# Graph attention on one core: combines moved behind the head, second maxima joined later, their store contiguous

## The reference

```python
seq = (x @ W_seq).reshape(N, H, DH)
score1 = jnp.einsum('nhd,d->hn', seq, a1)
score2 = jnp.einsum('nhd,d->hn', seq, a2)
scores = score1[:, :, None] + score2[:, None, :]
scores = jax.nn.leaky_relu(scores, negative_slope=ALPHA)
scores = scores + (1.0 - adj)[None, :, :] * MASK_VAL
attn = jax.nn.softmax(scores, axis=-1)
hidden = jnp.einsum('hij,jhd->ihd', attn, seq).reshape(N, D_IN)
hidden = hidden @ W_out + b_out
return jax.nn.elu(hidden)
```

## Time and profile before

| | us |
|---|---|
| median of 3 runs | 518.84 (518.45 to 519.27) |
| the profiled execution's own time | 522.9 |
| its span, first to last instruction | 521.2 |
| TensorE busy | 503.4 (97%) |
| VectorE busy | 459.6 (88%) |
| ScalarE busy | 433.7 (83%) |
| GpSimd busy | 34.8 (7%) |

### The profile page before, as it was taken

How to read it: one execution, slowest core, us unless ns; L and a number is a source line. 1 busy time by engine, 2 the same in 40 slices (tenths; PEclk the granted TensorE clock), 3 DMA queues, 4 the chain that set the end, 5 groups by cost and what they waited for, 6 DMA issues and landing times.

```text
span 521.2 us, 15251 instructions
## 1 busy us (share of the span) xinstructions
PE 503.4 (97%) x6744; PEld 456.7 (88%) x6744; DVE 459.6 (88%) x577; ACT 433.7 (83%) x462; POOL 34.8 (7%) x64
## 2 busy tenths in 40 slices
PE   7999999999999989999999999999999999899993
PEld 5788889999999889999999999999999999644542
DVE  3266899998999898999999999999998879988886
ACT  2477899798999887999999999999995989356664
POOL 3000000000000010000000000000000000035444
PEclk9899999999999989999999999999999999999998
DMA  7999995202020411201021120202202040015343
GB/s 258 395 302 344 333 332 142 86 3 82 3 83 2 115 38 55 83 3 82 3 83 31 54 83 3 83 1 83 79 7 82 3 143 3 1 62 159 122 141 122
DMA packets 31617, 53.28 MB, mean 102 GB/s; under 512 B 19392, under 2 KB 20672, under 8 KB 27584
## 3 DMA queue, kind: packets, MB, share of 16 engines
q1 hardware_dynamic: 31000, 51.79, 30.5%
q10 hardware_dynamic: 552, 0.52, 0.3%
HBM read 43.78 MB, written 4.33 MB: 92 GB/s over the span
## 4 chain that ended last, share of the span: by engine, by line
PE 80%; DVE 9%; DMA 4%; ACT 3%; issue 2%; POOL 0%; ACTq 0%; POOLq 0%; DVEq 0%
PE sums L475 35%; PE bank L489 19%; PE sums L568 10%; PE sums L400 6%; PE sums L416 4%; DVE tring L816 3%; ACT tring L614 2%; DVE tring L811 2%; DMA maxima<-Vp 2%; PE sums L387 1%; PE bank L416 1%; PE bank L556 1%; DMA Vp<-in_L_gnn_W_seq_dram 1%; DMA Vp<-maxima 1%; DVE Vp L792 1%
## 5 line engine op out<-in xcount | busy, mean ns | idle before, releaser
L614 ACT ACTIVATE tring<-abc,ab 128x2048 int8<-128x2048 f32 x150 | 292.2, 2019 | 2.0 <-PE sums L475 2.0
L475 PE MATMUL sums<-Vp,tring 128*128 128x132 f16 x4096 | 241.8, 221 | 3.5 <-issue 2.4
L475 PEld LDWEIGHTS sums<-Vp,tring 128*128 128x128 fp8e4 x4096 | 236.9, 98 | 5.5 <-issue 3.5
L816 DVE TENSOR_TENSOR tring<-adj,tring 128x1024 uint32<-128x1024 uint32 (+1 forms) x134 | 155.9, 1174 | 13.6 <-ACT tring L614 9.1
L489 PE MATMUL bank<-Vp,adj 128*128 128x132 f16 x2048 | 127.7, 222 | 2.1 <-DVE Vp L866 2.1
L489 PEld LDWEIGHTS bank<-Vp,adj 128*128 128x128 fp8e4 x2048 | 123.8, 97 | 2.3 <-DVE Vp L866 2.3
L811 DVE TENSOR_SCALAR tring<-abc,ab 128x2048 int8<-128x2048 f32 x90 | 115.5, 1283 | 0.0
L568 PE MATMUL sums<-abc,Vp 128*128 128x512 f32 (+1 forms) x136 | 57.5, 568 | 0.1
L568 PEld LDWEIGHTS sums<-abc,Vp 128*128 128x128 f32 x136 | 24.7, 190 | 22.7 <-issue 22.0
L652 ACT ACTIVATE low<-sums 128x33 f32<-128x33 f32 (+3 forms) x66 | 20.1, 393 | 24.1 <-PE sums L475 24.0
L592 ACT ACTIVATE tring<-Vp 128x2048 int8<-128x2048 f32 x16 | 30.6, 1911 | 1.2 <-DMA Vp<-in_adj_dram 1.2
(11 more groups left out here) (116 smaller groups left out, 369.7 us busy)
## 6 DMA issues: line engine op xcount, KB each, us to landing
Vp<-in_adj_dram SPq DMA_DIRECT2D x16, 1024.0 KB, 8.1
abc<-a_rows SPq DMA_DIRECT2D x15, 1024.0 KB, 4.8
abc<-in_x_dram SPq DMA_DIRECT2D x16, 256.0 KB, 7.4
Vp<-in_x_dram SPq DMA_DIRECT2D x16, 256.0 KB, 2.9
out_dram<-Vp SPq DMA_DIRECT2D x16, 256.0 KB, 2.0
abc<-in_L_gnn_W_out_dram SPq DMA_DIRECT2D x1, 1024.0 KB, 5.3
Vp<-in_L_gnn_W_seq_dram ACTq DMA_DIRECT2D x2, 256.0 KB, 5.4
Vp<-in_L_gnn_W_seq_dram SPq DMA_DIRECT2D x2, 256.0 KB, 6.1
```

Source lines behind the costliest of these rows:

```text
L475: mm = pe.matmul(bank[b][:, c * 2 * VW:(c + 1) * 2 * VW], slot(jt)[:, it * P:(it + 1) * P].bitcast(F8), Vp[:, h, jt, :, :], start=(jt == 0 ...
L614: return act.activation(slot(jt)[:, columns], row(h)[:, columns], ACT.Sign, bias=ab[:, jt, H + h:H + h + 1], scale=-1.0)
L816: return dve.tensor_tensor(words, edges, words, ALU.bitwise_and)
```

## The change

Three edits:
- The store of the second maxima writes `scratch2` in the order (partition, head), so each partition writes 8 successive values instead of 8 scattered ones. The maximum then reads `peaks` as "(q h)", with a step of 8 values between elements.
- The wait for the maxima, the maximum and the powers go from tile 7 to tile 11 of head 4, and `scale_factors` from tile 10 to tile 13.
- The combine of head k, k = 0 to 7, goes from tiles 11, 12 and 13 of head k + 4 to tiles 0, 2 and 3 of head k + 5. From head 12 on the old places hold (heads 8, 9 and 10), so head 12 has two combines and head 4 none.

```diff
--- before.py
+++ after.py
@@ -71,7 +71,8 @@
 VALUES_AT, HIGH_AT, LOW_AT = 1, 6, 9
 
 BEHIND_AT = (None, (6, 8)) + (range(6, NT),) * (H - 3) + ((5, 6, 8, 9),)
-FINISH_AT = (11, 12, 13)
+
+FINISH_AT, SOON_AT, LATER = (11, 12, 13), (0, 2, 3), 12
 
 THREE_AT = (9, 11, 15)
 
@@ -346,7 +347,7 @@
                 if h == 5:
 
                     sp.wait_ge(mx2_ready, 1)
-                    sp.dma_start(scratch2.rearrange("o (h p) -> (o p) h", p=P), mx2, allow_slow_non_contiguous=True).then_inc(mx2_stored, 16)
+                    sp.dma_start(scratch2.rearrange("o (p h) -> (o p) h", p=P), mx2).then_inc(mx2_stored, 16)
                     sp.wait_ge(mx2_stored, 16)
                     sp.dma_start(peaks, scratch2[0:1, :].partition_broadcast(P)).then_inc(peaks_loaded, 16)
                 sp.dma_start(row(h), scratch[h:h + 1, :].partition_broadcast(P)).then_inc(abc_loaded[h % 2], 16)
@@ -977,12 +978,12 @@
                     if h == 3 and jt == 14:
                         dve.wait_ge(mx2_part, 4)
                         dve.tensor_reduce(mx2, mxd.rearrange("p c k -> p k c"), AX.X, ALU.max).then_inc(mx2_ready, 1)
-                    if h == 4 and jt == 7:
+                    if h == 4 and jt == 11:
                         dve.wait_ge(peaks_loaded, 16)
-                        dve.tensor_reduce(mx2, peaks.rearrange("p (h q) -> p h q", q=P), AX.X, ALU.max).then_inc(peak_made, 1)
+                        dve.tensor_reduce(mx2, peaks.rearrange("p (q h) -> p h q", q=P), AX.X, ALU.max).then_inc(peak_made, 1)
                         dve.wait_ge(peak_made, 1)
                         powers(slice(HALF, H), mx2, 1)
-                    if h == 4 and jt == 10:
+                    if h == 4 and jt == 13:
                         scale_factors(1, slice(HALF, H))
                     if h == 5 and jt == 0:
                         dve.wait_ge(e_scaled, 4)
@@ -992,6 +993,8 @@
                             finish(step, h - GRP, 1, h - GRP)
                         dve.wait_ge(fin_step, 3 * (h - GRP + 1))
                         inverse(0, slice(0, NT), slice(0, H - GRP))
+                    if GRP < h <= LATER and jt in SOON_AT:
+                        finish(SOON_AT.index(jt), h - GRP - 1, 1, h - GRP - 1)
                     if jt == SUMS_AT[h]:
                         dve.wait_ge(low_copied, h)
                         if h > GRP:
@@ -1004,7 +1007,7 @@
                         if jt == VALUES_AT:
                             dve.wait_ge(v_ready, k)
                             values(k)
-                    if GRP <= h < H - 1 and jt in FINISH_AT:
+                    if LATER <= h < H - 1 and jt in FINISH_AT:
                         finish(FINISH_AT.index(jt), h - GRP, 1, h - GRP)
                     if h == H - 1 and jt in THREE_AT:
                         dve.wait_ge(joined, h)
```

## The result

The changed kernel is slower: median 523.2 us of 7 runs (521.91 to 524.6) against 519.27 us before, ratio 1.008, 95% interval [1.0062, 1.0099]. The forecast was 517.1 us. One of the 7 runs of the kernel before took 1828 us, which its median leaves aside.

What follows compares the result with a forecast made beforehand. TensorE bounds the kernel, busy 503.4 of 521.2 us, so only its waits count: 5.29 - 0.17 - 3.32 - 1.58 = 0.22, plus 1.48 of small waits, gain 1.70 from 518.84: 517.1 us; range 515.4 to 521.2.

Steps and rivals of the forecast that it cites:

- Head 4 and 5: VectorE's join of sums at 198.5 lets TensorE start head 5 at 199.9 (201.73 before), after 3.3 us idle.
- The reduction: VectorE's maximum over 1024 values in head 4, now read with a stride: 2.10 us instead of 1.22, a cost of 0.88.
- Stall (a): TensorE's gap after one product of head 4, until the maxima's store lands: 1.20 us lost, taken as the store's.
- Piece (c): Head 4's 64 products over the edges at half clock after a wait: 5.37 us instead of 3.79, 1.58 lost.
- Part 4: Combines moved behind the head, still ahead of the next join of sums: the work of one VectorE cycle stays.
- the 1.48 of small waits: TensorE's waits for VectorE ahead of heads 6, 8, 10 and 12, 0.37 us first, 1.48 in all: expected to go.
- The dependence: Last combine step is followed at once by the join overwriting its cab slot: 0.13 us, between 0 and 0.18.
- the third rival: Head 4's wait exists only in the profiled execution; new kernel slower by 2.3 to 3.0 us, 521.1 to 521.8; chance 25%.
- the 4.06 us: Excess of the profiled execution over the median; the store of 1024 pieces was called a likely place for it.
- the slow case: Outcome of the third rival: unprofiled, the old kernel reaches head 12 at 354.7, the new at 357.0 to 357.7.

Runs made afterwards that it cites:

- the join of sums at tile 2: Join of sums of heads 5 to 14 moved ahead of the join of tiles 2 and 3: alone on the kernel before 518.35 us, with store and maxima 516.13.
- maxima and join of sums: Kernel before with maxima joined at tile 11 and heads 5 to 14's join of sums at tile 2, store still scattered: 516.16 us, ratio 0.9937.

## Why the prediction was wrong, step by step

- **Head 4 and 5, right.** VectorE's join of sums was put 24.4 us behind the start of head 4 (198.5 less 174.12) and came at 24.35; head 5 was put at 25.8 and came at 25.77, with 3.05 us of idle for 3.32 and then the fall of the clock, 1.51 for 1.58. The reduction was put at 2.10 and took 2.03. The trace so bears out the small strided reductions of the earlier trace rows rather than the contiguous price. The rule on 16-byte lines in the Trainium skill's "SBUF — State Buffer" (Door 1: The DMA port swizzle) pointed the same way. The store was put at 2 us and took 1.4. Stall (a) was the store's.
- **Piece (c), over-counted.** The 1.58 us of half clock were taken as part of every execution. The second profile of the kernel before has nearly the same wait (1.88 us) without the fall, and then 4 to 5 takes 26.50. Against that profile the change wins 0.73 us at the start of head 5, and pays 1.51 behind it for a fall of the clock that the kernel before did not have there.
- **Part 4, the step that failed:** "So the work of one cycle stays" and, with it, "VectorE gets slack, so the 1.48 of small waits goes too". The count of VectorE's work was right, but work is not what bounds the cycle. The waits of 0.37 ahead of every second head were read as VectorE's saturation from the match of 22.31 and 22.32. They are the loop through ScalarE; the 22.31 is itself not pure work, as it holds short waits of 0.07 for ScalarE's masks. Two steps of the combine, moved from ahead of VectorE's wait for ScalarE's tile 1 to behind it, lengthen that loop by 1.23 us per two heads. From the start of head 6 to that of head 12, 6 x 22.31 = 133.9 us were forecast, 134.97 were there before, 138.73 (220.88 to 359.61) came. From the start of head 5 to that of head 12, against the second profile, it is 162.55 for 157.35 us: 3 x 1.23 for the loop and 1.51 for the clock. With the 0.73 won before it, the changed kernel loses 4.47 there. The medians differ by 3.9, and more than half of the executions of the kernel before have a lowered clock themselves.
- **The dependence** of the last step on the join was put at 0.13 us a head in VectorE's count; it measured 0.18 (0.80 instead of 0.62), and it lay on the loop.
- **The rivals.** The outcome, 0.8% slower, lies on the side of the third rival but not by its mechanism. That rival asked where the 4.06 us were and offered the wrong place; they lay in the start of the execution and in the clock, both of which that trace shows. That the combines' move might itself be the harm was no rival at all.
- **The range** ended at 521.2, inside the slow case that was worked out (521.1 to 521.8); the measured 523.2 lies beyond even that.

## What to carry to other kernels

An instruction that an engine executes ahead of a wait for another engine may be free, and the same instruction behind that wait may cost its whole length: before moving one, find on its engine the next wait on each side of both places. Where several engines show nearly the same period without idle, ask which wait passes the period on; follow it from the end of one stage over every engine to the start of a later one, over more than one stage if the waits alternate. And shorten what stands between the last wait and the signal that the bottleneck needs, as the join of sums at tile 2 did here.

## What the runs showed that was not expected

- **The clock falls after an idle time in some executions and not in others.** In the profiles it fell behind idle times of 2.12, 2.16, 2.35, 3.05, 3.38 and 3.44 us and held behind others of 1.88, 2.16 and 3.05. After 2.16 us of idle in head 4, 64 products took 5.47 us in one profile (store alone) and 3.96 in another (combines alone). After 3.05 us ahead of head 5 the clock was at 0.50 in the changed kernel and at full in the one with the combine moved in head 5 only. The fall costs 1.5 to 1.6 us each time. A single profile therefore does not tell what an idle time costs in the median.
- **A store of 4 KB held up TensorE.** In 1024 pieces it took 8.5 to 8.9 us, in 128 pieces 1.4, and near the end of the former TensorE stood between two products for 0.8 to 1.3 us. In five of the six profiles no gap follows during the 512 KB load behind it, in one (maxima and join of sums) a gap of 0.28.
- **The start differs between executions.** In the first profile of the kernel before, the clock from 10 to 20 us was 0.66 on average (1.00 in the second), and head 4 started 3.9 us later. One profiled execution per kernel showed a difference of 0.2 us in span where the medians differ by 3.9.
